# A three-layer cross network on one core: for the first tile, TensorE makes three chunks of turned x0 rows, and late stores, filter parts and the second tile's chunks change places

## The reference

```python
x0 = xk = inputs                      # b, 39, 16
for W in filters:                     # (39*39, 128), (128*39, 128), (128*39, 128)
    z = jnp.einsum('bfd,bgd->bfgd', x0, xk).reshape(b, f * g, d)
    cur = jnp.einsum('bpd,pm->bmd', z, W)
    outs.append(cur)
    xk = cur
z = jnp.sum(jnp.concatenate(outs, axis=1), axis=-1)   # b, 384
h = jnp.maximum(jnp.concatenate([z, dense_ctx], axis=1) @ W_top1 + b_top1, 0.0)
h = jnp.maximum(h @ W_top2 + b_top2, 0.0)
y = h @ W_top3                        # (512, 1)
```

## Time and profile before

| | us |
|---|---|
| timed runs, median of 3 | 677.55 (677.15 to 681.12) |
| profiled execution | 680.75 |
| its span | 678.8 |
| TensorE (PE) busy | 636.7 (94%) |
| VectorE (DVE) busy | 572.0 (84%) |
| GpSimd (POOL) busy | 533.8 (79%) |
| ScalarE (ACT) busy | 381.3 (56%) |
| granted TensorE clock, mean | 0.987 |

### The profile page before, as it was taken

One profiled execution on the slowest core, in us unless ns is written; L12 is line 12 of the kernel. 1 busy time (PEld: TensorE's weight loads), 2 busy tenths in 40 slices (PEclk: granted clock), 3 DMA queues, 4 the chain that ended last, 5 costly groups with the idle time before them and its releaser, 6 DMA issues.

```text
span 678.8 us, 11513 instructions
## 1 busy us (share of the span) xinstructions
PE 636.7 (94%) x2912; PEld 509.3 (75%) x2912; DVE 572.0 (84%) x1946; ACT 381.3 (56%) x1141; POOL 533.8 (79%) x528
## 2 busy tenths in 40 slices
PE   3278999999999999999999999999999999999998
PEld 1256867776777888888877888888887888888877
DVE  4457988998989898989879898989979898989870
ACT  0435565565757474756647474655657475655531
POOL 6754879999999989898978989897968989565420
PEclk9977999999999999999999999999999999999999
DMA  9423732302222222203131222203222130300000
GB/s 192 92 73 82 271 80 65 102 8 64 63 65 62 64 63 63 62 6 97 31 97 27 63 64 64 62 6 83 44 62 61 20 102 10 114 1 1 1 0 1
DMA packets 79940, 42.25 MB, mean 62 GB/s; under 512 B 56721, under 2 KB 64721, under 8 KB 79746
## 3 DMA queue, kind: packets, MB, share of 16 engines
q1 hardware_dynamic: 67246, 35.85, 20.1%
q10 hardware_dynamic: 7380, 4.38, 3.0%
q0 software_dynamic: 5248, 1.29, 2.0%
HBM read 39.52 MB, written 1.94 MB: 61 GB/s over the span
## 4 chain that ended last, share of the span: by engine, by line
PE 70%; POOL 8%; issue 8%; DVE 7%; SPq 4%; ACT 2%; DMA 0%; POOLq 0%; DVEq 0%; ACTq 0%
PE y L860 17%; PE y L862 16%; PE y L861 16%; DVE scaled L766 6%; PE side L867 4%; PE late L878 4%; PE acc L842 3%; PE acc L837 3%; PE acc L836 3%; POOL emb_quads L457 2%; SPq L377 2%; POOL z_parts L468 2%; ACT scaled L560 2%; POOL sum L483 2%; POOL sum L476 1%
## 5 line engine op out<-in xcount | busy, mean ns | idle before, releaser
L766 DVE SCALAR_TENSOR_TENSOR scaled<-y,x_rows,scaled 128x128 f32<-128x128 f32 x1728 | 466.6, 345 | 61.4 <-ACT scaled L560 50.9
L560 ACT ACTIVATE scaled<-y,x_rows 128x128 f32<-128x128 f32 x768 | 218.9, 367 | 213.6 <-PE y L862 188.5
L860 PE MATMUL y<-w_hi,x_parts 128*128 128x512 f32 (+1 forms) x640 | 277.3, 433 | 8.6 <-DVE scaled L766 2.5
L862 PE MATMUL y<-w_hi,x_parts 128*128 128x512 f32 (+1 forms) x640 | 249.8, 390 | 0.0
L861 PE MATMUL y<-w_lo,x_parts 128*128 128x512 f32 (+1 forms) x640 | 249.0, 389 | 0.0
L468 POOL TENSOR_TENSOR z_parts<-z,z_parts 117x512 fp32r<-117x512 f32 (+1 forms) x107 | 138.7, 1296 | 37.7 <-ACT z_parts L519 36.0
L457 POOL DMA_INDIRECT emb_quads<-in_small_tables_dram,quad_rows x144 | 139.4, 968 | 27.1 <-issue 14.6
L860 PEld LDWEIGHTS y<-w_hi,x_parts 128*128 128x128 f32 x640 | 121.5, 190 | 46.2 <-DVE scaled L766 17.4
L862 PEld LDWEIGHTS y<-w_hi,x_parts 128*128 128x128 f32 x640 | 121.0, 189 | 25.3
L861 PEld LDWEIGHTS y<-w_lo,x_parts 128*128 128x128 f32 x640 | 121.9, 190 | 19.0
L483 POOL TENSOR_TENSOR sum<-sum,scaled 128x512 f32<-128x512 f32 x63 | 81.8, 1299 | 25.1 <-DVE scaled L766 23.8
(11 more groups left out here) (91 smaller groups left out, 347.9 us busy)
## 6 DMA issues: line engine op xcount, KB each, us to landing
z<-x_turned SPq DMA_DIRECT2D x311, 78.0 KB
x_three<-x_turned SPq DMA_DIRECT2D x48, 78.0 KB
x_turned<-emb_quads SPq DMA_DIRECT2D x156, 8.0 KB
w_sb<-in_w_dram SPq DMA_DIRECT2D x1, 2496.0 KB, 9.4
emb_quads<-in_small_tables_dram,quad_rows POOLq DMA_INDIRECT x144
s_sb<-in_w_dram ACTq DMA_DIRECT2D x12, 160.0 KB
x_turned<-emb_singles SPq DMA_DIRECT2D x89, 2.0 KB
x_turned<-emb_quads SPq DMA_DIRECT2D x64, 2.0 KB
```

The source lines that it names most:

```text
L560: done = act.activation(scaled[:, k % 2, BY_ACT.index(j), i * M:(i + 1) * M], y2[n % RING][:, i * M:(i + 1) * M], ACT.Copy, scale=x0_rows[ ...
L766: dve.scalar_tensor_tensor(part, y2[n % RING][:, i * M:(i + 1) * M], x0_f, part, ALU.mult, ALU.add).then_inc(terms_in, 1)
L860: pe.matmul(dst, x1_hi[:, t % 2, cols], hi, start=True, stop=False)
L862: pe.matmul(dst, x1_lo[:, t % 2, cols], hi, start=False, stop=True).then_inc(y_ready, 1)
```

## The change

- **TensorE makes chunks 0 to 2 of tile 0.** `turn_x0` holds four 0/1 matrices from an array that the kernel already had as an input. After the stores and after x0 is loaded, four fp32 matmuls pick rows: three give the turned rows of chunks 0, 1, 2 in the banks `y2[0]` to `y2[2]`, the fourth gives `three_ps`. DVE then multiplies `y2[c]` with `x0_three` for these chunks. The nine DMAs for chunks 0 to 2 and ScalarE's copy of tile 0 go; `keep_warm(12)` becomes `keep_warm(5)`.
- **Loads of tile 0** now: x0 three times, chunks 3 and 4 on ScalarE's queue; chunks 5 and 6 and the quarters on SP.
- **Stores.** SP: first copies of the singles, quads 8, 4, 7, 0, 5. ScalarE: the second copy of the singles' one field before the dense part; quad 4's and 0's second copies; quads 1, 2, 3, 6 whole. Tile 1's singles are stored between ScalarE's high parts of tile 0.
- **Second filter.** Pieces 0 and 1 are loaded by SP ahead of its stores, 2 and 3 by ScalarE. The high parts stand between ScalarE's stores. DVE's low parts first wait for the last fetch of tile 0.
- **Tile 1:** its first two chunks are multiplied at slots 7 and 10 (5 and 9 before), its `three_ps` copy stands at slot 6 (4 before).

```diff
 TURNS = F // 2 + 1
+
+BY_PE = 3
 SEL_REP = 0
...
 CHUNKS_AT = (0, 4, 8, 12, 16, 20, 24)
-FIRST_CHUNKS_AT = (5, 9, 13, 17, 21, 24, 27)
+FIRST_CHUNKS_AT = (7, 10, 13, 17, 21, 24, 27)
 HIGH_LAG = 2
...
 THREE_AT = 38
-FIRST_THREE_AT = 4
+FIRST_THREE_AT = 6
 DIAG_AT = (1, 2, 4, 5, 7, 8, 10, 11)
...
         w0_raw = s_sb[:, 1, 2 * C0:3 * C0, :]
+        turn_x0 = s_sb[0:F, 1, 3 * C0:3 * C0 + 1 + BY_PE, :]
...
-            return 16 * turns(c) * (u + 1)
+            return 16 * turns(c) * (u if c < BY_PE else u + 1)
...
-        def store_singles(queue, u, copies):
+        def store_singles(queue, u, copies, which=range(len(SINGLES))):
             g, q = u // TPG, u % TPG
             queue.wait_ge(singles_in[g], 16 * len(SINGLES))
-            for i, f in enumerate(SINGLES):
+            for i in which:
+                f = SINGLES[i]
                 for at in [(f, F + f)[c] for c in copies if c == 0 or f < TURNED]:
...
+        def three(queue, u):
+            if u == 2:
+                queue.wait_ge(rows_up, BY_PE)
+                queue.wait_ge(prod, BY_PE)
+            if u >= 2:
+                queue.wait_ge(three_up, u - 1)
+            for r in range(3):
+                queue.dma_start(x0_three[F * r:F * r + F, u % 2, :], x0_dram[u, 0:F, :]).then_inc(three_in[u % 2], 16)
+
...
         def _(sp):
-            def stores(u, copies):
-                if u != 1:
-                    store_singles(sp, u, copies)
+            def stores(u):
+                if u > 1:
+                    store_singles(sp, u, (0, 1))
                 for i in QUAD_ORDER:
-                    store_quad(sp, u, i, copies)
+                    store_quad(sp, u, i, (0, 1))
...
-            def three(u):
-                if u >= 2:
-                    sp.wait_ge(three_up, u - 1)
-                for r in range(3):
-                    sp.dma_start(x0_three[F * r:F * r + F, u % 2, :], x0_dram[u, 0:F, :]).then_inc(three_in[u % 2], 16)
-
             sp.dma_start(ids_sb[:, 0, :], ids[0:P, :]).then_inc(ids_in, 16)
...
             sp.dma_start(ids_sb[:, 1:GROUPS, :], ids[P:B, :].rearrange("(g p) f -> p g f", p=P)).then_inc(rest_ids_in, 16)
+            for j in (0, 1):
+                load_filter(sp, j)
+            store_singles(sp, 0, (0,))
+            for i in (8, 4, 7, 0, 5):
+                store_quad(sp, 0, i, (0,))
             for u in range(TILES):
-                stores(u, (0,) if u == 0 else (0, 1))
+                if u > 0:
+                    stores(u)
                 sp.wait_ge(stored[u % 2], 16 * STORES * (u // 2 + 1))
-                three(u)
-                for c in (1, 2, 4, 6) if u == 0 else range(C0):
+                if u > 0:
+                    three(sp, u)
+                for c in (5, 6) if u == 0 else range(C0):
                     if u > 0:
...
-            def three(u):
+            def second_filter_high(j):
+                act.wait_ge(w1_in[j], 64)
+                copy(w1_hi[:, j:F:4, :], w1_raw[:, j:F:4, :]).then_inc(w1_hi_in, 1)
+
+            def three_to_psum(u):
                 act.wait_ge(three_in[u % 2], 48 * (u // 2 + 1))
...
             act.dma_start(ident[:, :], identity[:, 0:P]).then_inc(weights_in, 16)
+            act.dma_start(turn_x0.rearrange("p a b -> p (a b)"),
+                          selectors[0:F, SEL_A * P:(SEL_B + BY_PE) * P]).then_inc(turn_in, 16)
             act.dma_start(wt1_sb[0:16, 3, :], wt1[3 * P:FEATURES, :]).then_inc(dense_in, 16)
...
             act.dma_start(bt1_sb[:, :], bt1).then_inc(dense_in, 16)
-            for j in range(W1_PIECES):
+            for j in (2, 3):
                 load_filter(act, j)
...
             copy(w0_hi[:, :, :], w0_raw).then_inc(w0_hi_in, 1)
+            store_singles(act, 0, (1,))
             act.wait_ge(dense_in, 48)
...
                 act.activation(dense_h1[:, c, :], y2[c][:, 0:LEFT], ACT.Identity, bias=bt1_sb[:, c:c + 1]).then_inc(dense_up, 1)
-            store_singles(act, 0, (1,))
-            for i in QUAD_ORDER:
-                if any(len(rows) > 1 for _, _, _, rows in runs(QUADS[i])):
-                    store_quad(act, 0, i, (1,))
-                if i == 0:
-                    store_singles(act, 1, (0, 1))
-            for j in range(W1_PIECES):
-                act.wait_ge(w1_in[j], 64)
-                copy(w1_hi[:, j:F:4, :], w1_raw[:, j:F:4, :]).then_inc(w1_hi_in, 1)
+            second_filter_high(0)
+            second_filter_high(1)
+            store_quad(act, 0, 4, (1,))
+            store_quad(act, 0, 0, (1,))
+            second_filter_high(2)
+            for i in (1, 2, 3, 6):
+                store_quad(act, 0, i, (0, 1))
+            second_filter_high(3)
             act.wait_ge(stored[0], 16 * STORES)
-            turned_rows(act, 0, 0)
-            three(0)
+            three(act, 0)
             turned_rows(act, 0, 3)
+            turned_rows(act, 0, 4)
             for c in range(C0):
                 high_part(0, c)
-                if c == 0:
-                    turned_rows(act, 0, 5)
+                if 0 < c <= len(SINGLES):
+                    store_singles(act, 1, (0, 1), (c - 1,))
             x1_high(0)
...
                     if t == 0 and s == FIRST_THREE_AT:
-                        three(1)
+                        three_to_psum(1)
                     if t + 2 < TILES and s == THREE_AT:
-                        three(t + 2)
+                        three_to_psum(t + 2)
                     if g > 0:
...
             def product(u, c):
-                if c == 0:
+                if u == 0 and c == 0:
+                    dve.wait_ge(three_in[0], 48)
+                if c == (0 if u > 0 else BY_PE):
                     dve.wait_ge(three_up, u + 1)
...
                 k = depth(c)
-                dve.tensor_tensor(z[0:k, c, :], z[0:k, c, :], three_ps[0:k, :], ALU.mult).then_inc(prod, 1)
+                if u == 0 and c < BY_PE:
+                    dve.wait_ge(rows_up, c + 1)
+                    dve.tensor_tensor(z[0:k, c, :], y2[c][0:k, :], x0_three[0:k, 0, :], ALU.mult).then_inc(prod, 1)
+                else:
+                    dve.tensor_tensor(z[0:k, c, :], z[0:k, c, :], three_ps[0:k, :], ALU.mult).then_inc(prod, 1)
...
             dve.tensor_tensor(w0_lo[:, :, :], w0_raw, w0_hi[:, :, :].bitcast(F32), ALU.subtract).then_inc(w0_lo_in, 1)
+
+            dve.wait_ge(quad_in[QUAD_ORDER[-1]][0], 16)
             for i in range(W1_PIECES):
...
             pe.wait_ge(stored[0], 16 * STORES)
-            keep_warm(12)
+            keep_warm(5)
+            pe.wait_ge(three_in[0], 48)
+            pe.wait_ge(turn_in, 16)
+            pe.wait_ge(dense_up, H1 // P)
+            for c in range(BY_PE):
+                pe.matmul(y2[c][0:3 * F, :], turn_x0[:, 1 + c, 0:3 * F], x0_three[0:F, 0, :], start=True, stop=True).then_inc(rows_up, 1)
+            pe.matmul(three_ps[0:3 * F, :], turn_x0[:, 0, 0:3 * F], x0_three[0:F, 0, :], start=True, stop=True).then_inc(three_up, 1)
             for c in range(C0):
```

2 lines of the change are left out of this document (added).

## The result

The changed kernel takes 680.19 us (median of 19 runs, 678.51 to 681.8), the kernel before 677.57 (19 runs, 675.94 to 681.3). The ratio is 1.0029, with a 95% interval of 1.0016 to 1.0041: 0.3% slower, where 671.8 was forecast.

A forecast was written before the change was run, and what follows sets the result against it. TensorE, busy 94% of the span, was taken as the bound, so start-up time counts fully. Gains of 1.4 + 1.2 + 2.3 + 0.9 = 5.8 us off the 677.55 median gave 671.8 us; 8-in-10 range 667.5 to 676.3.

The forecast's parts named there:

- Term 1: Start, tile 0's stores to DRAM: the wait for them passed at 26.3 instead of 27.71 us, gain 1.4 us.
- The bound named first: Tile 0's stores: embedding fetches land at about 22.2 us, so the stores can't end before 24.5.
- the third rival: Start: ScalarE's filter copies hold its DMAs (28.6 us), stores come no earlier, no change, near 676 us; chance 0.10.
- Term 2: Start, load of x0: kept at 4.46 us, bounds 3.5 and 5.5, so x0 is back at 30.8.
- Term 3: From x0 to layer 2, with TensorE's selections and seven contractions: 15.0 us against 16.2, gain 1.2 us.
- less: Selections stay at the low clock throughout, two contractions at half rate: gain only 2.9 us, 674.7 us; chance 0.15.
- Terms 4 and 5: Tile 0: the stall for tile 1's x0 goes, gain 2.3 us; the low clock behind it partly goes, gain 0.9.
- More: Start and tile 0: the clock rises early and stays, gain 8 to 10.1 us, 667.5 to 669.5 us; chance 0.25.
- Slower: Start: sync's filter load lands late, holding ScalarE's stores and every later step; 1% slower if at 32.1 us; chance 0.05.

The follow-up runs named there:

- e15: The changed kernel run once more without edits, on another chip; one execution, 682.79 us, layer 2 at 52.53 us.
- e3: The kernel before with the change's store and filter order, fetch wait and tile 1 slots, all chunks still by DMA, keep_warm(12); 678.75 us, ratio 0.9997.
- e4: The changed kernel with stores, filter and DVE's wait as in the kernel before; 680.43 us, ratio 1.0034 to before.
- e12: The changed kernel with each of the four selections done twice into the same bank; one execution, 690.27 us.
- e1: The changed kernel with keep_warm(12) instead of keep_warm(5) ahead of the selections; 677.52 us, ratio 0.9985 to before.
- e5: The changed kernel with 30 keep-warm matmuls ahead of the wait for the stores and 18 behind it, instead of 5; 677.1 us, ratio 0.9971 to before.
- e2: The kernel before with only tile 1's slots moved (copy to 6, first chunks to 7 and 10); 679.08 us, ratio 1.0014.
- e6: The changed kernel with 30 and 18 keep-warm matmuls plus a scrap matmul behind each pair of last_begins; 675.08 us, ratio 0.9956 to before.
- e8: The kernel before with 30 and 18 keep-warm matmuls (none and 12 before); 680.33 us, ratio 1.0032.
- e10: The kernel before with only the later layers' weight loads moved one tile on, behind tile 2's loads; 679.1 us, ratio 0.9949.
- e11: The kernel before, unedited, profiled once more; one execution, 685.6 us, layer 2 at 50.68 us.

## Why the prediction was wrong

The sum forecast 674.9 us for the profiled execution, and it was 680.57: 5.7 us more. Layer 2 begins 5.4 us later than forecast (51.16 for 45.8), tiles 0 and 1 gain 2.6 more (5.8 for 3.2), and the last part costs 2.9 that no term had. On top comes the step to the median, below.

**Term 1, the stores: wrong, 1.8 us.** Forecast 26.3, measured 28.10 (27.69 in e15). The bound named first, the fetches, is the one that holds, and it was priced too low in three places. The issue that the prediction called the last fetch of tile 0 (18.33) is the eighth of nine; the ninth ends at 20.68 after. It lands 4.4 us later where 2.4 was taken, between the 1.8 and 2.9 of the loads of the first 4 us, and the last store counts as done 2.7 us after its issue and not 1.8. 20.7 + 4.4 + 0.3 + 2.7 is 28.1. The order of the stores didn't move that: e3 and e4 pass the wait at 28.8 and 28.2. It is what the third rival said would come (the stores come no earlier), but not by its reason: ScalarE's queue issued its last stores from 24.08 on, while the third filter copy ran from 23.93, so the copies didn't hold them.

**Term 2, the load: right.** 4.54 us, kept at 4.46.

**Term 3, x0 to layer 2: the step that failed.** Its 15.0 us were 18.5. The price of the selections at the low level was right (7.1 for 7.3), and so was the tail (1.50). Wrong was "I take 4.5 us low ... then the rest at double rate". The selections stayed low for all 7.11 us (1.2 us more), and the two contractions behind them took 2.30 and 2.07 us where a cycle of 1.15 was counted (2.1 more). The rival called "less" had this at 0.15. The 4.5 us came from the low stretches of tile 0, which are layer 2's matmuls of 128 rows and came after a pause; no row of before showed a clock rising under a selection. e12 shows it: 14 us of selections alone left the level low, and in e1 and e5, where the clock had risen under the keep-warm matmuls, the four took 3.6 to 3.7 us. The Trainium skill (TensorE: Matmul & The Clock Gate, "What's actually happening") describes the low rate as the default which the engine's activity releases. The trace agrees for the keep-warm matmuls and the contractions (0.63 us each, then 0.40), and doesn't for these selections of 39 rows in fp32, which keep TensorE busy for 7.11 of 7.11 us and leave the level low; what distinguishes them for the chip isn't shown, since rows and type weren't changed apart.

The cut from keep_warm(12) to keep_warm(5), which the prediction passed over with "which nobody waits for", was thus the dearest line of the change: restored alone (e1) it brings layer 2 from 51.16 to 45.16 and the median from 680.2 to 677.5. It rests on a misread row. The prediction took the twelve matmuls of before (4.76 us, 0.40 each) as low throughout. 0.40 is a mean over both levels: matmuls of this size start 0.43 us apart at the low one and 0.23 at the upper, and the first contraction after them was at the upper level in before. Only then did the level fall, and it was low until 41.8:

```profile
34.55 0.40 PE L837 MATMUL acc<-z_parts,w_lo 117*128 117x512 f32 x1
...
35.10:41.83 6.73, 4.79 (x10) 3.33 (x11) 4.83 (x8) 2.49 (x4) 1.70 (x2) 0.50 0.42 125
```

So the twelve had been raising the clock in before, and the five of the change (2.47 us) didn't.

**Terms 4 and 5, the stall and the clock behind it: right, and too small.** The gain is 5.2 us in tile 0 (36.86 for 42.07) and 0.5 in tile 1, for 3.2 forecast. ScalarE finds tile 1's x0 there at 57.79, and no stretch of the tile is low. Before, two stretches were low; the prediction had left the first one (48.34 to 52.40) in and taken a third of the second. Most of this gain needs no TensorE chunks: in e2 a shift of two slots alone brought tile 0 to 38.8.

**What no term had: tile 2's x0.** The sum assumed that an earlier layer 2 moves everything behind it. It would have met ScalarE's next wait. In the kernel after tile 2's copy runs at 86.58 unhindered, because layer 2 had begun late; in e5, 5.5 us earlier, it waits for 3.24 us and in e2 for 5.64. The earlier trace rows end ahead of these loads, and the prediction's working didn't have the weights in front of them. Against 36.7 without it, tile 1 took 1.3 us (e5), 5.6 (e6) and 5.1 (e2) more with that wait, and nothing in e1, where it lasted 2.16 us. So a start at 45.8 could have been worth up to 5 us less than counted.

**The step to the median.** The prediction took the gain off the median although the sum was made against an execution 3.2 us above it, as if the same surplus were in both kernels. That execution of before had low stretches in its contractions and twice in tile 0, and a mean granted clock of 0.987; of 69 other executions of before on the chips of e1 to e8, four had as little. Kernels made from before with almost the same start (e2, e3, e10) begin layer 2 at 44.7 to 45.7, and not at 48.4 or, as in e11, 50.7. So what Terms 4 and 5 removed was probably in part a surplus that the median of before doesn't have. With two profiles of before, both about 3 us above the median, this isn't shown.

**The other rivals.** "More" (the clock up early) is what e1 and e5 show with more keep-warm work, and even then the medians are 677 and not 667.5 to 669.5; the two terms that were missing are part of that. "Slower" by a late filter didn't occur: ScalarE stood for at most 0.22 us ahead of a filter copy. That the change came out slower at all goes with the cold selections: it is there in e4 and gone in e1. That the profiled pair comes out even is chance: a later start and a longer last part happen to cancel what tiles 0 and 1 gained.

## What to carry to other kernels

Work that TensorE takes over in a start-up phase has to be priced at the level of the clock that the phase leaves it with, and what stands ahead of it (here filler matmuls) belongs to that price: look at the durations of one and the same matmul, not only at the clock column. Before an earlier start is credited, walk the queue that feeds the next tiles, to the second and third hand-over, and ask which transfer becomes the bound; here an edit of one line that moves five weight loads was worth 0.5%, and the whole rework of the start lost 0.3%. Make the sum against an execution that is near the median, or take two profiles.
